# Four small moves in a four-layer attention and expert kernel: one load, shared sums, the order of some operations, and the order of the stores

## The reference

```python
x = x + L0_xattn(norm(x), ctx)      # 8 heads in windows, output bias bo
x = x + L0_ffn(norm(x))             # 8 experts, top 1
x = x + L1_xattn(norm(x), ctx)      # 16 heads
x = x + L1_ffn(norm(x))             # 16 experts, top 3, weighted
x = x + L2_xattn(norm(x), ctx)      # 16 heads, causal, output bias bo
x = x + L2_ffn(norm(x))             # ternary weights, relu squared
x = x + L3_xattn(norm(x), ctx)      # 16 heads, masked
y = x + magnitude(x) * directions[tile]          # 64 tiles
out = (y - mean(y)) / sqrt(var(y) + eps) * norm_gamma + norm_beta
```

## Time and profile before

| | us |
|---|---|
| median of 3 runs (lowest, highest) | 573.29 (572.55, 574.57) |
| the profiled execution, its own time | 575.11 |
| its span from first to last instruction | 573.4 |
| TensorE busy | 428.6 (75%) |
| VectorE busy | 333.1 (58%) |
| ScalarE busy | 238.8 (42%) |
| GpSimd busy | 234.8 (41%) |
| mean granted TensorE clock | 0.79 of full speed |

### The profile page before, as it was taken

The page is one execution under the profiler, slowest core; times in us unless marked ns, Lnnn a source line. Parts: engine busy times, 40 slices in busy tenths (PEclk is TensorE's granted clock), DMA queues, the critical chain, the costliest instruction groups (busy, mean ns, idle before and its releaser), DMA issues.

```text
span 573.4 us, 9996 instructions
## 1 busy us (share of the span) xinstructions
PE 428.6 (75%) x2628; PEld 355.2 (62%) x2628; DVE 333.1 (58%) x1130; ACT 238.8 (42%) x635; POOL 234.8 (41%) x294
## 2 busy tenths in 40 slices
PE   5879678997898876529984749568899999982550
PEld 4768667995677775219973738436676667771440
DVE  6665355656786436215531317277776767858887
ACT  2332224664544212126752426334565646562221
POOL 2513730036327573720454341747811334533214
PEclk9795568999988557559995859778899999995555
DMA  6999546882651110212442323211000000000002
GB/s 188 299 403 388 122 123 212 290 284 54 203 187 46 34 48 16 80 37 70 130 117 61 98 60 89 74 32 39 0 1 2 1 0 1 2 1 1 0 1 73
DMA packets 60548, 55.42 MB, mean 97 GB/s; under 512 B 11922, under 2 KB 46446, under 8 KB 60366
## 3 DMA queue, kind: packets, MB, share of 16 engines
q1 hardware_dynamic: 53214, 43.64, 23.7%
q0 software_dynamic: 4736, 9.71, 5.8%
q10 hardware_dynamic: 2544, 1.44, 0.8%
HBM read 24.10 MB, written 30.67 MB: 96 GB/s over the span
## 4 chain that ended last, share of the span: by engine, by line
PE 44%; DVE 19%; another core or an unknown queue 9%; issue 9%; ACT 6%; POOL 5%; DVEq 5%; DMA 2%; SPq 2%; ACTq 0%; POOLq 0%
PE bank L2286 9%; PE bank L2273 8%; PE bank L2143 4%; PE bank L2127 3%; PE bank L2265 3%; PE bank L2132 2%; PE bank L2158 2%; PE bank L1982 2%; POOL wall L676 2%; DVE stats L846 2%; ACT xn L1654 2%; DVE e_sb L1256 1%; PE bank L2115 1%; PE bank L2416 1%
## 5 line engine op out<-in xcount | busy, mean ns | idle before, releaser
L1748 ACT ACTIVATE r<-bank,b 128x128 f32<-128x128 f32 x218 | 65.8, 365 | 56.1 <-PE bank L2273 33.8
L630 POOL TENSOR_TENSOR rstd<-veps,mhalf 128x4 f32<-128x4 f32 x32 | 33.8, 1056 | 132.0 <-DVE veps L851 131.6
L2286 PE MATMUL bank<-wall,r 128*128 x436 | 71.6, 299 | 20.9 <-ACT r L1748 17.6
L2286 PEld LDWEIGHTS bank<-wall,r 128*128 128x128 f32 x436 | 60.9, 207 | 23.9 <-issue 23.0
L2273 PE MATMUL bank<-on,e_sb 128*128 128x128 f32 x348 | 61.0, 310 | 9.0 <-issue 6.1
L676 POOL DMA_INDIRECT vZ<-outbuf,slots x40 | 39.2, 979 | 67.5 <-DMA outbuf<-h_sb 49.2
L1321 DVE TENSOR_TENSOR h_sb<-bank,b2all 128x128 f32<-128x128 f32 x86 | 25.0, 290 | 66.6 <-PE bank L2286 47.5
L2273 PEld LDWEIGHTS bank<-on,e_sb 128*128 128x128 f32 x348 | 51.5, 216 | 10.8 <-issue 10.8
L649 POOL DMA_INDIRECT outbuf<-h_sb,slots x48 | 46.5, 970 | 23.0 <-issue 15.1
L2143 PEld LDWEIGHTS bank<-vB,eT 128*128 128x128 f32 x384 | 52.7, 213 | 0.0
L2143 PE MATMUL bank<-vB,eT 128*128 128x36 f32 x384 | 52.5, 287 | 0.0
(11 more groups left out here) (306 smaller groups left out, 876.3 us busy)
## 6 DMA issues: line engine op xcount, KB each, us to landing
outbuf<-zero SPq DMA_DIRECT2D x17, 1024.0 KB
wall<-in_w SPq DMA_DIRECT2D x4, 2048.0 KB, 13.8
outbuf<-h_sb SPq DMA_DIRECT2D x66, 64.0 KB
h_sb<-outbuf SPq DMA_DIRECT2D x63, 64.0 KB
h_sb<-rowbuf SPq DMA_DIRECT2D x23, 64.0 KB
outbuf<-h_sb POOLq DMA_DIRECT2D x20, 64.0 KB, 2.0
x<-in_x ACTq DMA_DIRECT2D x4, 256.0 KB, 6.3
b2all<-in_L_ffn_b SPq DMA_DIRECT2D x1, 1024.0 KB, 15.5
```

Of the source, the lines that this page charges most:

```text
L630: r = nc.gpsimd.tensor_tensor(rstd[:, at], veps[:, at], mhalf[:, 0:W], ALU.pow)
L1748: i = a.activation(hT[:, u * 512 + c * P:u * 512 + (c + 1) * P], bank[2 + u][:, c * P:(c + 1) * P], ACT.Relu, bias=b1[l][:, bass.ds(e * C ...
L2286: y = mm(bank[6 + s % 2][:, 0:P], hT[:, (s % 2) * 512 + c * P:(s % 2) * 512 + (c + 1) * P], wall[:, bass.ds(e * n + (WHALF + c * P), P)], ...
```

## The change

Five edits. (1) `expert_biases(1)` and its wait move from behind the small loads to in front of them. (2) `add_last` on GpSimd takes only the last two tiles of batch 3; the first two are summed by VectorE in `add_first`, in period 5 of part 4. (3) Batch 1's third pass and statistics move behind the first `max_sub` of part 4. (4) On GpSimd the power for batch 1 moves ahead of batch 2's last three gathers, and the power for batch 3 ahead of the second bias addition. (5) Batch 1's gamma and beta are done by VectorE (`scaled_rows(1)`), ahead of batch 2's centring, and the stores go in the order 0, 1, 2, 3.

```diff
--- before.py
+++ after.py
@@ -59,6 +59,7 @@
 ROUND = 1.5 * 2.0 ** 30
 RING = 4
 LATE = (0, 4, 8)
+BY_VECTOR = 2
 REGION = T + 1
 GRID = 16
 TAB = 4 * GRID + 1 + D
@@ -490,6 +491,8 @@
             expert_weights(1)
             for i in range(9):
                 clear(1, i)
+            sp.wait_ge(s_vwP, B)
+            expert_biases(1)
             load(s_ca, wo[2][:, :], A["wo2"])
             for l in (4, 6):
                 load(s_ca, wk[l][:, :], A[f"wk{l}"])
@@ -522,8 +525,6 @@
             load(s_c7, oscale[:, :], rows(A["L3_ffn_output_scale"]))
             load(s_c7, gamma[:, :], rows(A["L3_ffn_norm_gamma"]))
             load(s_c7, beta[:, :], rows(A["L3_ffn_norm_beta"]))
-            sp.wait_ge(s_vwP, B)
-            expert_biases(1)
 
             def zero_rows():
 
@@ -594,11 +595,11 @@
                     if l == 1 and s >= PLACES and s % 2 == 0 and 9 + (s - PLACES) // 2 < 17:
                         clear(3, 9 + (s - PLACES) // 2)
 
-            for b in (0, 2, 1, 3):
-                if b < 2:
-                    sp.wait_ge(s_op7, b + 1)
+            for b in range(B):
+                if b == 0:
+                    sp.wait_ge(s_op7, 1)
                 else:
-                    sp.wait_ge(s_o7, b - 1)
+                    sp.wait_ge(s_o7, b)
                 sp.dma_start(out[b].rearrange("(w p) f -> p w f", p=P),
                              tile_of(y7, b, S).rearrange("p (w f) -> p w f", w=W)).then_inc(s_out, 16)
             sp.wait_ge(s_out, 16 * B)
@@ -681,10 +682,11 @@
                 pool.wait_ge(s_gsub, 2)
                 for i in range(UNDER_WAY[3]):
                     pool.wait_ge(*gathered(3, last_of(3, 3) - i))
-                rows = yg[3][3][:, 0:W * K * D].rearrange("p (w k f) -> p w k f", w=W, k=K)
-                own = tile_of(x, 3, S).rearrange("p (w f) -> p w f", w=W)
-                weights = gk[:, :].rearrange("p (k t) -> p t k", k=K)[:, 3 * W:4 * W]
-                nc.gpsimd.tensor_tensor(rows, rows, weights.unsqueeze(3).to_broadcast([P, W, K, D]), ALU.mult).then_inc(s_sum, 1)
+                n = W - BY_VECTOR
+                rows = yg[3][3][:, BY_VECTOR * K * D:W * K * D].rearrange("p (w k f) -> p w k f", w=n, k=K)
+                own = x[:, (3 * W + BY_VECTOR) * P:4 * W * P].rearrange("p (w f) -> p w f", w=n)
+                weights = gk[:, :].rearrange("p (k t) -> p t k", k=K)[:, 3 * W + BY_VECTOR:4 * W]
+                nc.gpsimd.tensor_tensor(rows, rows, weights.unsqueeze(3).to_broadcast([P, n, K, D]), ALU.mult).then_inc(s_sum, 1)
                 for k in range(K):
                     pool.wait_ge(s_sum, k + 1)
                     nc.gpsimd.tensor_tensor(own, own, rows[:, :, k], ALU.add).then_inc(s_sum, 1)
@@ -741,15 +743,16 @@
             gather(3, 0)
             gather(3, 1)
             power(16)
-            gather(3, 2)
+            gather(3, 2, 0, 9)
             power(17)
+            gather(3, 2, 9)
             gather(3, 3, 0, 8)
             power(18)
             gather(3, 3, 8)
             add_last()
             add_bo(0)
+            power(19)
             add_bo(1)
-            power(19)
             add_bo(2)
             add_bo(3)
             for n in range(20, 24):
@@ -832,7 +835,6 @@
             last_rows(0)
             last_power(2)
             last_power(3)
-            last_rows(1)
 
 
         @block.vector
@@ -1281,6 +1283,8 @@
                 if l == 4 and t == 2:
                     add_experts(3, 2, (2,))
                     stats_of(norm_no(4, 2), 2)
+                if l == 4 and t == 5:
+                    add_first()
                 if l == 4 and t == 7:
                     dve.wait_ge(s_sum, TOPK[3] + 1)
                     stats_of(norm_no(4, 3), 3)
@@ -1308,6 +1312,19 @@
                             i = v.scalar_tensor_tensor(tile_of(x, t), tile_of(yg[3][b], w * K + k), gk[:, k * T + t:k * T + t + 1],
                                                        tile_of(x, t), ALU.mult, ALU.add)
                 i.then_inc(s_gad, 1)
+
+            def add_first():
+
+                K, first = TOPK[3], last_of(3, 2) + 1
+                for i in range(UNDER_WAY[3]):
+                    dve.wait_ge(*gathered(3, first + BY_VECTOR * K - 1 - i))
+                for k in range(K):
+                    if k:
+                        dve.drain()
+                    for w in range(BY_VECTOR):
+                        t = 3 * W + w
+                        v.scalar_tensor_tensor(tile_of(x, t), tile_of(yg[3][3], w * K + k), gk[:, k * T + t:k * T + t + 1],
+                                               tile_of(x, t), ALU.mult, ALU.add)
 
             def moe(l):
                 E, C = MOE[l]
@@ -1351,9 +1368,6 @@
                         add_experts(3, 1, ((s + 4 - NS) // 2,))
                 for s in range(NS - LAG, NS):
                     add_bias(s, experts[s])
-                if l == 3:
-                    add_experts(3, 1, (2,))
-                    stats_of(norm_no(4, 1), 1)
 
             def v_loads(src, E):
 
@@ -1430,7 +1444,10 @@
                     dve.wait_ge(s_r5, b * 4 + (c + 1))
                     v.tensor_tensor(tile_of(h_sb, (b % 2) * 4 + c, S), r, r, ALU.mult).then_inc(s_q5, 1)
 
-            for t in range(-1, 18):
+            period(4, -1)
+            add_experts(3, 1, (2,))
+            stats_of(norm_no(4, 1), 1)
+            for t in range(18):
                 period(4, t)
             squares(0)
             squares(1)
@@ -1578,6 +1595,17 @@
                 for w in range(b * W, (b + 1) * W):
                     i = v.scalar_tensor_tensor(tile_of(y7, w), tile_of(y7, w), rs7[:, w:w + 1], tile_of(xb7, w), ALU.mult, ALU.add)
                 i.then_inc(s_o7, 1)
+
+            def scaled_rows(b):
+
+                def rows7(buf):
+                    return tile_of(buf, b, S).rearrange("p (w f) -> p w f", w=W)
+
+                dve.wait_ge(s_n7, b + 1)
+                v.tensor_tensor(rows7(y7), rows7(y7), gamma[:, :].unsqueeze(1).to_broadcast([P, W, D]), ALU.mult)
+                dve.drain()
+                dve.wait_ge(s_xb, b + 1)
+                v.tensor_tensor(rows7(y7), rows7(y7), rows7(xb7), ALU.add).then_inc(s_o7, 1)
 
             for t in range(-1, 19):
                 period(6, t)
@@ -1603,6 +1631,7 @@
             magnitudes(1)
             last_stats(2 * W, 3 * W)
             last_stats(3 * W, 4 * W)
+            scaled_rows(1)
             centred(2)
             dve.drain()
             last_rows(2)
```

## The result

The changed kernel took 576.68 us (median of 22 runs, 571.52 to 586.13) beside 574.35 us (22 runs, 567.62 to 580.50) for the kernel before: ratio 1.0101, 95% interval 1.0065 to 1.0138. A ratio here leaves out runs more than 1.5% above the fastest of their kernel, which trims the slow side of a kernel that scatters widely (here 7 of the 22 runs before and 4 of the 22 after); so medians of all runs stand beside each ratio. By medians the change cost 2.3 us, 0.4%. It was slower, and neither "no change" nor 573.5 us.

What follows compares the result with a forecast made beforehand. No engine was taken as full; the chain hops between engines, each hop the later of two arrivals. 0 (biases) + 0.65 (layer 4) - 0.45 (end) = +0.2 on 573.29 gave 573.5 us, chance 0.41; range 570.2 to 576.9.

Steps and rivals of the forecast that it cites:

- Biases first: Start of the first expert layer: loading expert biases earlier is hidden by SyncE's tile-list wait; value 0, bounds -0.3 and +0.7 us.
- End of the second expert part: Shorter gather burst brings ScalarE's copy 3.5 us sooner; score wait and softmax step spend it, batch 1's variances 0.6 later.
- the second rival: End of second expert layer: lateness not tied to gathers, variances 4.0 us later; +3.6 in all, 576.9 us; chance 0.22.
- step A: GpSimd's layer 4 powers, batch 0 to 1, including the second expert part's end; batch 1's variances were forecast 0.6 us later.
- GpSimd's chain: Layer 4: starts 0.6 later, gathers +3.75, halved sums -2.9, earlier power -0.8; net +0.65 us, range -0.2 to +2.2.
- Step C: GpSimd's layer 4 powers, batch 2 to 3: halved product and sums 2.9 us less, earlier power of batch 3 0.8 back.
- Step B: GpSimd's layer 4 powers, batch 1 to 2: three more gathers of 1.25 us, +3.75.
- VectorE as the other arrival: Layer 4, before batch 3's statistics: VectorE arrives at 406.5, at most 408.9, so GpSimd at 407.35 still ends last.
- less up to 2.4 us of waits that it had in between: Layer 4: VectorE's delay of 3.15 plus 2.1 us shrinks by up to 2.4 as earlier waits absorb it.
- the first rival: Behind layer 4's sums, 411 to 418: a shorter wait lets TensorE keep its clock; 2.8 us less, 570.7; chance 0.27.
- The end: Last 10 us: VectorE's two new operations +1.6, batch 2's scalings -2.04; -0.45 us, bounds -0.8 and +0.6.
- The third and fourth rivals: The end: powers hold up VectorE's new operations, 574.5; or scalings are held up by something else, 575.5; chance 0.05 each.

Runs made afterwards that it cites:

- the changed kernel's third: The changed kernel, nothing edited, measured a third time beside the kernel before, on the first kind of chip: 576.62 us, ratio 1.0018 (0.9976 to 1.0059).
- all of layer 4: Kernel before plus shared sums, batch 1's power before three gathers, its sums after first softmax step, batch 3's power before a bias addition: 584.45 us, ratio 1.0016.
- earlier sums: The changed kernel with VectorE's six new sums one period earlier, in period 4 of layer 4: 581.90 us, ratio to the kernel before 1.0040 (1.0001 to 1.0078).

## Why the prediction was wrong

**Biases first: about right.** 0 was predicted. SyncE's wait of 2.2 us in place of 2.7 covers it, and the two ratios (0.9972, 1.0003; medians 1.1 us below and 2.1 above) show no clear cost. What I can't place are the 2.88 us that the changed kernel had lost by 358. From the first powers of part 2 to the last of part 3 (91.6 us before, 96.9 in the changed kernel) kernels with the edit took 93.6 and 94.0 on one chip where those without took 90.7 and 90.8, on a second 94.6 to 95.9 against 92.3, and on a third 95.1 against 93.1 to 96.2. But on the first of these chips the stretch is longer only because it starts earlier with the edit (131.3 and 131.9 against 134.5 and 134.5); it ends alike, at 225.0 and 225.9 against 225.1 and 225.3. So the loss of the profiled pair didn't come again there. What made it stays open.

**End of the second expert part: right.** The copy 1.5 us behind the ninth gather refutes the second rival (a tail not tied to the gathers), and step A grew by 0.55 in the profiled pair where 0.6 was forecast. Over the traces of the first kind with unchanged code A is 23.4 to 25.6, with the edit 23.9 to 24.9: nothing of the 3.5 us of the shorter burst is left there, as forecast, though that scatter hides anything under 2 us. On the second kind the edit is worth 1.2 us in A.

**GpSimd's chain: right in its terms.** Product and sums took 3.90 (1.48, and 2.34 with gaps), forecast 3.9. Step C with the shared sums and no moved gathers is 14.1 to 14.2 against 17.6: 3.5 less, forecast 2.9 + 0.8. Step B grew by 2.5 to 3.4, a little less than the 3.75 of three gathers. The forecast had these two nearly cancel; with the moved gathers, C didn't shrink as it should.

**The step that failed: VectorE as the other arrival.** The prediction let it come to batch 3's statistics at 406.5 to 408.9 and wrote that the middle lies ahead of GpSimd's 407.35. The middle is 407.7, behind it; only the early end lies ahead, so its own numbers didn't give "GpSimd still ends last". In the profiled trace, counted from the first power, VectorE came at 411.66 - 2.88 = 408.8, the late end. That is 2.8 behind the 406.00 of before, and less the 0.8 that came back as forecast it is the measured +2.0 in place of +0.65.

The term that failed is "less up to 2.4 us of waits that it had in between". The waits before were 0.72 and 1.70. Without the moved gathers they are absorbed, as the prediction wanted: VectorE has no wait over 0.3 us from 378 to 406, its six sums take 1.98 at 397.07, ahead of the product at 399.30, and it comes to the statistics at 403.48. In the changed kernel 0.74 and 2.07 are left, and nothing was absorbed. The prediction priced the new gap behind 382 at 3.15 us; of the clock it said only, in the first rival, that this gap lies "where TensorE was slow before too", and put it at nothing. The trace shows what it cost beyond that: behind the gap TensorE's granted clock fell, to 0.50 where the wait of 2.07 begins, where before it had been at 1.00. From the turning over of batch 2's rows to the end of their scores the same products took from 403.79 to 408.45, 4.66 us, and from 397.52 to 400.36, 2.84, in the kernel without the moved gathers. So by an estimate from these rows 1.8 of the 2.07 us are the clock's; without them VectorE would have come within 0.3 us of GpSimd's 409.56.

In three other traces of the first kind (the changed kernel's third, all of layer 4, earlier sums) step C was 4 to 5 us longer still. There hand-overs of TensorE in the last four gathers are late on top, by up to 6 us on ScalarE and 0.8 to 2.2 on VectorE, and in two of the three VectorE's new sums fell beside GpSimd's product. A+B+C is 49.7 without the moved gathers and 55.2 to 60.9 with them and the shared sums.

What is shown and what not: that the moved gathers (with the two moves that belong to them) cause the loss is shown on three chips, by 569.71 against 576.62, by 577.12 for the shared sums against 584.45 for all of layer 4, and by the moved gathers alone, 1.0070 (1.0036 to 1.0103). That the clock falls with them is shown by the table. That both go by VectorE's wait of 4.3 us is what the traces fit, and only half tested; how the loss divides among clock, late hand-overs and collision, no run separates. The nearest is the second kind of chip, where no wait ends "remote" and the sums met nothing: there C is 15.09 with the moved gathers and 13.89 without. The prediction named all three ingredients, a clock that hangs on a wait, late hand-overs in a burst and one engine held up by another, but for other places, and its last sentence named the run of 11 gathers as a danger without giving it a price. Its range ended at +2.2 for this place; the two pairs of traces of one kind put it at +2.0 (55.24 against 53.25) and +6.0 (59.91 against 53.90).

**The end: right in sign, small in size.** Two operations of 0.69 ahead, scalings 3.18 to 1.14: from the variances to the last scaling 6.70 became 6.03, that is -0.67, forecast -0.45. The third and fourth rivals are out: with GpSimd's two operations gone the scalings take what batch 3's always took. GpSimd's power beside the new operations took 1.38 in place of 1.04 and held nothing up. By the Trainium skill (SBUF — State Buffer, "SBUF: two separate sides") whichever of a VectorE operation with two SBUF inputs and a GpSimd operation that reads SBUF starts first has the shared ports, and the other waits for all of it. The collisions agree (six sums in 5.05 and 5.42 in place of 1.98, behind a product that GpSimd had started 0.5 and 0.2 us earlier); the four centrings of 1.13 beside a power still don't.

**The first rival, the clock,** came true as a mechanism and was mis-sized: in the 7 us behind the sums the granted clock was 1.00 in place of 0.54, TensorE got 43 products through in place of 31, but the way from batch 3's power to the second one of layer 5 shrank only from 15.43 to 14.43. Over the traces with unchanged code behind that power it is 13.6 to 16.2, so even that 1.0 is within scatter. The same mechanism acted the other way ahead of this place, in step C, where no rival looked for it.

**Sum.** Forecast +0.2: about 0 from the biases, +0.65 from layer 4, -0.45 from the end. Measured in traces: layer 4 +2.0 and +6.0, the end -0.7. For the profiled pair the span grew by 2.7: 2.9 before layer 4's first power, 2.0 in A to C, 1.0 back behind it, 0.7 back at the end and 0.5 back in smaller pieces. The medians are 2.3, 2.9 and 5.6 us above before on the first kind.

**A better kernel.** The changed kernel with gathers and batch 1's sums left as before took 569.71 us where before took 573.75 and the changed kernel 576.62; its ratio to before, 0.9976 (0.9942 to 1.0009), doesn't prove a gain on the first kind, though by medians it is 4.0 us. On the second it is 0.9831 and 0.9874, both intervals below 1; there A+B+C is 2.7 us shorter than in the changed kernel, but the medians are alike (501.61 and 501.97).

## What to carry to other kernels

Moving work ahead of a transfer that another engine waits for cost that engine more than its wait here: what stood behind it slipped, and what it slipped into set the price. A new gap of one engine was also a gap of TensorE's, and behind that the clock was lower where it had been full before; so look at the clock behind every gap that a change makes, not only behind those that it closes. Price the later arrival at a join with the waits that it will meet at its new time, not with those of the old trace, and take the late end when it slips towards a burst. Check, too, that the middle of a range lies on the side that the argument needs. And share sums between VectorE and GpSimd only where their halves don't run at the same time: step C became 3.5 us shorter so, and the sums took 3.1 to 3.4 us more where they met.

## What the hardware showed

The two kinds of chip differ in one kind of wait, and in the mean granted clock (0.78 to 0.80, and 0.85, of full speed in the traces). In each of the 14 traces of the first kind, VectorE and ScalarE have 22 to 33 waits that end "remote", 93 to 139 us in all; in the six of the second kind there is none. The kernel with the moved gathers alone ran on both. On the first kind two of its groups of such waits are (total us, times, longest)

```profile
DVE h_sb L1322 <- remote: 36.1, 9, 10.0
...
ACT r L1749 <- remote: 14.7, 7, 4.2
```

and at the end of the second expert part the timelines of VectorE, ScalarE and GpSimd show

```profile
373.95 0.51 DVE L1322 TENSOR_TENSOR h_sb<-bank,b2all 128x128 f32<-128x128 f32 x2 [6.23 <-remote]
...
373.94 0.62 ACT L1749 ACTIVATE r<-bank,b 128x128 f32<-128x128 f32 x2 [2.21 <-remote]
...
371.23 0.94 POOL L676 DMA_INDIRECT vZ<-outbuf,slots  x1 [0.30 <-issue]
```

On the second kind VectorE, beside gathers of the same 0.94, shows

```profile
299.92 0.29 DVE L1322 TENSOR_TENSOR h_sb<-bank,b2all 128x128 f32<-128x128 f32 x1 [0.85 <-PE bank L2287]
300.95 0.29 DVE L1322 TENSOR_TENSOR h_sb<-bank,b2all 128x128 f32<-128x128 f32 x1 [0.75 <-PE bank L2287]
```

On the first kind both engines restart together 1.8 us behind the last gather; on the second VectorE's waits end with TensorE's products (0.85 and 0.75 us) right through the gathers. The second expert part, busy us and clock, first and then second kind (columns as in the earlier trace rows):

```profile
228.00:356.00 128.00, 85.22 (x565) 73.48 (x565) 43.63 (x165) 52.87 (x180) 52.40 (x65) 0.77 0.28 80
```

```profile
208.00:293.00 85.00, 79.38 (x568) 70.77 (x567) 44.68 (x169) 54.19 (x185) 52.48 (x66) 0.91 0.44 123
```

The same work takes 128 us and 85 us, with busy times nearly equal: 43 of the some 70 us by which the kinds differ. In the places shown the held-up hand-overs come beside indirect transfers issued by GpSimd; whether the transfers hold them up, and why one kind of chip has them and the other not, no run shows. This change was by medians 1.9% faster on a chip of one kind and 0.4 to 1.0% slower in three comparisons on the other.
